# Routing of a mixture-of-experts layer: two-byte lookup tables with the choices innermost, totals taken as one more rank, and the first four gathers issued by the routing block

## The reference

```python
def _L0_ffn_ref(x, W_gate, b_gate, W_e, b_e):
    TOP_K = 2
    logits = x @ W_gate + b_gate
    _, top_idx = jax.lax.top_k(logits, TOP_K)
    y_all = jax.nn.relu(jnp.einsum('bsd,edh->bseh', x, W_e) + b_e)
    y = jnp.take_along_axis(y_all, top_idx[..., None], axis=2)
    return y.mean(axis=2)
...
x = x + 0.5 * _L0_ffn_ref(_layernorm(x, axis=-1), ...)
x = x + _L0_attn_ref(_layernorm(x, axis=-1), ...)
x = x + 0.5 * _L0_ffn_ref(_layernorm(x, axis=-1), ...)
```

## Time and profile before

| | |
|---|---|
| median of 3 runs | 1069.3 us (1067.76 to 1070.01) |
| the profiled execution, its time | 1067.34 us |
| the profiled execution, its span in the trace | 1065.6 us |
| first expert layer in the trace: routing, experts | 0 to about 105 us, about 106 to about 240 us |
| second expert layer: routing, experts | about 784 to 912 us, 913 us to the end |
| TensorE busy over the span | 82% |
| granted TensorE clock, mean | 0.918 of full |

### The profile page before, as it was taken

One profiled execution on the slowest core, in us unless ns is written; L12 is line 12 of the kernel. 1 busy time (PEld: TensorE's weight loads), 2 busy tenths in 40 slices (PEclk: granted clock), 3 DMA queues, 4 the chain that ended last, 5 costly groups with the idle time before them and its releaser, 6 DMA issues. The chain is left out here.

```text
span 1065.6 us, 20204 instructions
## 1 busy us (share of the span) xinstructions
PE 876.0 (82%) x6688; PEld 640.8 (60%) x6689; DVE 670.0 (63%) x1295; ACT 443.9 (42%) x817; POOL 355.4 (33%) x340
## 2 busy tenths in 40 slices
PE   3676799993699987838999999999959984699994
PEld 3564688872477776725555555555437863488873
DVE  7977244431788988837777777777527676344431
ACT  3332233331134433334777777777723430133331
POOL 5540677764012321220000000000014440477764
PEclk9997799997799999977999999999979895699997
DMA  8873578863226488664666666554047882378773
GB/s 262 284 261 119 163 143 150 149 120 62 46 85 188 149 217 203 164 201 119 146 147 136 135 138 138 132 137 119 25 134 245 291 277 99 75 141 158 145 134 49
DMA packets 123099, 162.08 MB, mean 152 GB/s; under 512 B 16864, under 2 KB 74336, under 8 KB 122752
## 3 DMA queue, kind: packets, MB, share of 16 engines
q1 hardware_dynamic: 105168, 123.85, 41.5%
q0 software_dynamic: 17856, 37.25, 18.8%
HBM read 97.44 MB, written 67.37 MB: 155 GB/s over the span
## 5 line engine op out<-in xcount | busy, mean ns | idle before, releaser
L825 DVE TENSOR_REDUCE att_part<-att_s_ps 128x2 f32<-128x1024 f32 (+2 forms) x160 | 195.5, 1225 | 67.4 <-PE att_s_ps L673 67.0
L787 ACT ACTIVATE att_prob<-att_st_ps 128x512 f32<-128x512 f32 x320 | 173.7, 595 | 78.4 <-PE att_st_ps L699 78.0
L143 PE MATMUL exp_z_ps<-ex_w_hi,exp_xT_hi 128*128 x312 | 132.7, 425 | 3.4 <-issue 2.1
L144 PE MATMUL exp_z_ps<-ex_w_lo,exp_xT_hi 128*128 x312 | 126.0, 404 | 0.0
L145 PE MATMUL exp_z_ps<-ex_w_hi,exp_xT_lo 128*128 x312 | 125.7, 403 | 0.0
L1459 DVE TENSOR_TENSOR exp_xT_lo<-exp_t_ps,exp_xT_hi 128x512 fp32r<-128x512 f32 x78 | 54.0, 692 | 109.3 <-ACT exp_xT_hi L1445 109.3
L1452 ACT ACTIVATE exp_y<-exp_y 128x512 f32<-128x512 f32 x72 | 45.5, 632 | 170.5 <-DVE exp_y L1471 170.5
L1387 POOL DMA_INDIRECT exp_xg<-xn,ex_token_of x78 | 77.9, 999 | 89.5 <-SPq L1359 61.4
L1094 POOL TENSOR_TENSOR ex_w_lo<-ex_bias,ex_w_hi 128x1024 fp32r<-128x1024 f32 x32 | 75.8, 2368 | 90.0 <-ACT ex_w_hi L1198 89.9
L712 PE MATMUL att_pv_ps<-att_prob,att_v_sb 128*32 128x256 f32 (+2 forms) x1280 | 101.4, 391 | 1.8 <-ACT att_oT L792 1.8
L637 POOL CAST att_m_parts<-att_part 128x28 fp32r<-128x28 f32 x32 | 6.6, 206 | 271.5 <-DVE att_part L829 271.5
(11 more groups left out here) (198 smaller groups left out, 1725.1 us busy)
## 6 DMA issues: line engine op xcount, KB each, us to landing
ex_bias<-in_L_ffn_W_e SPq DMA_DIRECT2D x32, 512.0 KB, 6.5
v_vals<-qkv_vals SPq DMA_DIRECT2D x16, 512.0 KB, 2.8
q_parts<-qkv_partq SPq DMA_DIRECT2D x32, 256.0 KB, 3.3
k_parts<-qkv_partk SPq DMA_DIRECT2D x32, 256.0 KB, 3.7
att_v_sb<-v_vals SPq DMA_DIRECT2D x32, 256.0 KB, 3.5
ex_bias<-in_L_attn_hidden_states SPq DMA_DIRECT2D x8, 512.0 KB, 4.1
acc<-ex_bias SPq DMA_DIRECT2D x8, 512.0 KB, 6.5
xn<-route_xn SPq DMA_DIRECT2D x8, 512.0 KB, 4.9
```

The source lines that it names most:

```text
L143: nc.tensor.matmul(out, x_hi[:, s], w_hi(c), start=(c == 0), stop=False)
L144: nc.tensor.matmul(out, x_hi[:, s], w_lo(c), start=False, stop=False)
L787: nc.scalar.activation(prob[n % 2][:, col:col + 512], st_ps[(e + half) % 3][:, :], ACT.Exp).then_inc(exp_done, 1)
L825: nc.vector.tensor_reduce(out, src, X_AXIS, ALU.max, negate=True).then_inc(red_done, 1)
```

## The change

- The two tables have all operands in two-byte elements and the 32 choices as the innermost index. `at_tile` is written by three operations of VectorE on two tensors each; its second part is preset by POOL with the tiles' numbers. `at_col` is written by 4 operations of 1024 elements (8 choices each) in place of 32 of 128. PE's 32 matmuls read every 32nd element of `at_tile` and every 8th of `at_col`, and wait once for 8 of them.
- The totals are no longer 16 matmuls of their own: the rank matmuls run one tile further.
- `token_of` is written right behind the matmuls and ahead of `before_of`. POOL issues gathers 0 to 3 at the end of the routing block, from `ex.gather`; the expert block starts at gather 4.
- The identity is built once, and the six `prime` transfers are issued in the routing block, ahead of the first `w_lo`.
- `xn` of the routing block and the first four gather buffers share the memory `ex.rows`. `at_col` lies in the idle `wo_turned` in the first layer and in `o` and `xT` in the second.

```diff
@@ class Experts
+        self.rows = m.sb("rows", [P, C, D]) if rows is None else rows
+        self.ident = m.sb("ident", [P, P])
+        self.prime = m.sb("prime", [1, ADD_RING * 16])
...
+    def gather(self, nc, xn_dram, s, xg):
+        nc.gpsimd.indirect_dma_start(out=xg, out_offset=None, in_=xn_dram[:, :],
+                                     in_offset=bass.IndirectOffsetOnAxis(ap=self.token_of[:, s:s + 1], axis=0)
+                                     ).then_inc(self.gathered[s % ADD_RING], 16)
@@ route_block, gpsimd
-            nc.gpsimd.iota(n_col[:, :], [[1, P]], channel_multiplier=0, **small).then_inc(const_done, 1)
+            nc.gpsimd.iota(n_col[:, :, :], [[1, P], [0, COLS]], channel_multiplier=0, **small).then_inc(const_done, 1)
+            nc.gpsimd.iota(at_tile[:, 1, :, :], [[1, TAB], [0, 2 * TILES]], channel_multiplier=0, **small).then_inc(const_done, 1)
...
+            for r in range(ADD_RING):
+                nc.gpsimd.dma_start(ex.prime[0:1, r * 16:(r + 1) * 16], ident[0:1, 0:16]).then_inc(ex.added[r], 16)
+            for r in range(ADD_RING):
+                pool.wait_ge(ex.added[r], 16)
             for n in range(TILES):
                 pool.wait_ge(w_hi_done, n + 1)
...
+            pool.wait_ge(tr_done, TILES)
+            for par in range(2):
+                pool.wait_ge(xn_stored[par], 16 * (PAIRS // 2))
+            pool.wait_ge(token_done, 1)
+            for s in range(C):
+                ex.gather(nc, xn_dram, s, ex.rows[:, s, :])
@@ route_block, tensor
+            nc.tensor.matmul(total_ps, ones_bf[:, :], both[:, 0:2 * E], start=False, stop=False, skip_group_check=True)
             for s in range(1, TILES):
-                last = nc.tensor.matmul(rank_ps[:, s * 2 * E:TE2], ones_bf[:, :], both[:, 0:TE2 - s * 2 * E], start=False,
-                                        stop=(s == TILES - 1), skip_group_check=True)
-            for s in range(TILES):
-                last = nc.tensor.matmul(total_ps, ones_bf[:, :], both[:, s * 2 * E:(s + 1) * 2 * E],
-                                        start=(s == 0), stop=(s == TILES - 1))
+                last = nc.tensor.matmul(route_ps[:, s * 2 * E:TE2 + 2 * E], ones_bf[:, :], both[:, 0:TE2 - (s - 1) * 2 * E],
+                                        start=False, stop=(s == TILES - 1), skip_group_check=True)
...
             for n in range(2 * TILES):
-                pe.wait_ge(onehot_done, n + 1)
-                nc.tensor.matmul(id_ps, at_col[:, n % COL_RING, :], at_tile[:, n, :, :].rearrange("p a s -> p (a s)"),
-                                 start=(n == 0), stop=(n == 2 * TILES - 1)).then_inc(ids_done, 1)
+                if n % COLS == 0:
+                    pe.wait_ge(onehot_done, n // COLS + 1)
+                last = nc.tensor.matmul(id_ps, at_col[n // COLS][:, :, n % COLS],
+                                        at_tile[:, :, :, n].rearrange("p a s -> p (a s)"), start=(n == 0), stop=(n == 2 * TILES - 1))
+            last.then_inc(ids_done, 1)
@@ route_block, vector
-            chain(nc.vector.tensor_tensor(at_tile[:, :, 0, :], slot_hi[:, :, :].to_broadcast(every),
...
-            for n in range(2 * TILES):
-                if n >= COL_RING:
-                    dve.wait_ge(ids_done, n - COL_RING + 1)
-                nc.vector.tensor_scalar(at_col[:, n % COL_RING, :], n_col[:, :], slot_lo[:, n:n + 1], None,
-                                        ALU.is_equal).then_inc(onehot_done, 1)
+            chain(nc.vector.tensor_tensor(at_tile[:, 0, :, :], at_tile[:, 1, :, :], by_choice(slot_hi[:, :], TAB), ALU.is_equal))
+            chain(nc.vector.tensor_tensor(at_tile[:, 1, :, :], at_tile[:, 0, :, :], by_choice(n_token_row[:, :], TAB), ALU.mult))
+            chain(nc.vector.tensor_tensor(at_tile[:, 2, :, :], at_tile[:, 0, :, :], by_choice(n_token_tile[:, :], TAB), ALU.mult))
+            for j in range(2 * TILES // COLS):
+                nc.vector.tensor_tensor(at_col[j], n_col[:, :, :],
+                                        by_choice(slot_lo[:, j * COLS:(j + 1) * COLS], P), ALU.is_equal).then_inc(onehot_done, 1)
...
+            dve.wait_ge(ids_done, 1)
+            chain(nc.vector.tensor_copy(found[:, :, :], ids))
+            nc.vector.scalar_tensor_tensor(ex.token_of[:, :], found[:, 2, :], float(P), found[:, 1, :],
+                                           ALU.mult, ALU.add).then_inc(token_done, 1)
@@ expert_block, gpsimd
-            gather(0)
-            make_identity(nc, pool, ident, zeroed, ident_done)
-            for s in range(1, AHEAD):
+            for s in range(C, AHEAD):
                 gather(s)
```

82 lines of the change are left out of this document (36 added, 46 removed).

## The result

The changed kernel takes 1078.15 us (median of 4 runs, 1076.38 to 1079.51); the kernel before took 1069.19 in the same session. The ratio is 1.0096, with a 95% interval of 1.0070 to 1.0121: slower, where I had forecast 1063.8 and a gain. The profiled execution has a span of 1076.1 us against 1065.6, so 10.5 us are to be explained.

A forecast was written before the change was run, and what follows sets the result against it. Bound: routing's serial VectorE-TensorE-VectorE chain, then TensorE in the expert block. Layer one -3.2 - 1.95 + 2.2 = -2.95, layer two -3.2 + 0.6 = -2.6, together -5.5: profiled 1067.3 to 1061.8, median 2.0 above, 1063.8; range 1058.5 to 1069.

The forecast's parts named there:

- Only then does POOL reach the barrier ... With the old 1.29 TensorE enters at 6.5.: Routing's end: fourth gather issued 5.2 us after `token_of`, barrier 1.29 later; first expert product z at 9.1, both layers.
- used to share the queues with the 2 MB of biases: Layer one, `token_of` to first expert product z: gathers formerly shared queues with biases; 9.1 against 11.05 us gains 1.95.
- Half of it gives 12.5 for the first `w_lo` ... So 2.8 - 0.57 = 2.2 reach the gate.: Layer one start: half the 2.6 us queue congestion delays priming; fourth weight load 2.8 late, 2.2 us lost.
- ScalarE's slack: Layer one start: ScalarE's copy of the last tile but one started 0.57 us after rounding, subtracted from the 2.8 delay.
- Neither row is near, so I take the middle, 0.165.: TensorE's 32 table matmuls with strided operands: 0.165 us each, between 0.103 packed and 0.228 for four-byte transposes.
- the upper row: Upper price for the 32 matmuls: transposes of 128 four-byte columns at the same 0.50 clock, 0.228 us each.
- T to `token_of`: Start of the tables (T) to `token_of` written: 9.45 us in place of 12.43, in each layer.
- strided reads cost as four-byte ones: Rival on the 32 matmuls: 0.228 us each, 2.0 more per layer, 1067.8 in all; chance 0.10.
- hide behind POOL's gathers: Behind `token_of`, VectorE's `before_of` operations and `row_of` take about 3 us, covered while POOL issues gathers.
- VectorE's terms: Tables on VectorE: three `at_tile` operations at 0.82 us each, 2.6 in all; four `at_col` at 0.72 with gap.
- T+3.3: Tables: the first of four `at_col` operations is done 3.3 us after their start, and the 32 matmuls begin.
- the totals, -0.2: Logits to tables, each layer: 256 columns added to the rank matmuls and 16 matmuls gone, 0.2 us less.

The follow-up runs named there:

- one gather: Changed kernel with only gather 0 in the routing block, gathers 1 to 3 at the start of the expert block; 1069.61 us in a single run.
- `iota`s: Changed kernel with four 128 x 480 number writes by GpSimd where the four gathers were issued, all first gathers in the expert block; 1078.57 us, one run.
- no bias load: Changed kernel with layer one's 2 MB bias load issued by SyncE at the start of the expert block, behind the barrier; 1071.65 us, one run.
- the gathers put back: Changed kernel with gathers 0 to 3 issued at the start of the expert block again; 1074.01 us, ratio 1.0062 to the kernel before.
- both loads put back: Changed kernel with the six priming transfers behind the `w_lo` operations and all first gathers in the expert block; 1068.97 us, ratio 1.0026 to the kernel before.
- both loads put back and `before_of` moved: Kernel with both loads put back, and the five `before_of` operations ahead of VectorE's wait for the 32 matmuls; 1067.76 us, ratio 1.0018 to the kernel before.

## Why the prediction was wrong

The span came out 16.0 us above the forecast (+10.5 against -5.5). Three steps failed. They make 16.7 us in these two traces, and the rest of the table takes 0.7 back.

**"Only then does POOL reach the barrier ... With the old 1.29 TensorE enters at 6.5."** This is the largest, 7.3 + 2.7 = 10.0 us over the two layers. I took the issue of the last gather for the end of GpSimd's block. The block ended only when its transfers had landed: 4.05 us after the end of the last issue, not 1.29. That is 2.7 per layer, which is what layer two missed by (11.78 against 9.1) and layer one too once the bias load is away (11.83). In layer one I had argued that the gathers would gain because they "used to share the queues with the 2 MB of biases". They still did: the load waits for the last 16 transposes, ended at 110.04, and was issued at 110.08, while gather 1 was. Another 4.6. That the barrier waits for the landings of GpSimd's own transfers is shown by three runs (one gather: 3.67; `iota`s: 2.09 and 1.75; no bias load: 4.10 and 4.10) and by the packets: in six kernels with gathers in front of the barrier it opened 1.55 to 1.76 us behind their last packet, in both layers of each. A transfer of SyncE's queue did not hold it: before, the bias load was issued at 104.38 and its packets ran until 111.40, over the barrier at 106.30, and so it was with the gathers put back. Which wait in the block's end does it, the profile does not show.

**"Half of it gives 12.5 for the first `w_lo` ... So 2.8 - 0.57 = 2.2 reach the gate."** Mechanism right, size wrong: 6.1, 3.9 more, in this trace. Over the six kernels with this start it is 2.6 to 6.1 against the one trace of before, 4.3 in the mean, so about 2 of the 3.9 repeat and the rest may be luck. The first `w_lo` began at 13.65, 1.15 later than I said: GpSimd was free at 6.69 and not 6.0, six issues took 3.2 and not 3.0, and the last landing 3.76 more and not 3.5. The fourth weight load came at 18.31 against 14.52, so 3.8 late and not 2.8. That is 1.0 of the 3.9; the other 2.9 is what followed. The delay did not travel unchanged to the last load, as I had it, but grew on the way, to 5.1 at the fifth (23.62 against 18.52) and 6.4 at the last (75.42 against 69.06); the logits were 6.1 late, so ScalarE's slack took 0.3 off it and not 0.57. SyncE's queue stood behind its wait, the transfer engines were idle for 4 us, and VectorE waited 20.1 us for inputs where it had waited 4.3. That the idle transfer engines are why the delay grew fits these rows, but no run isolates it. The `iota`s, on which 2.4 us of my delay rested, cost nothing where the priming doesn't stand behind them, although `n_col` took 1.92 and not 1.0: GpSimd then waits 1.92 us for the weights.

**"Neither row is near, so I take the middle, 0.165."** The matmuls cost 0.208, between my price and the upper row (0.228). That is 1.4 us per layer, and it explains all of the miss in T to `token_of` (10.86 against 9.45; VectorE's part agreed). My rival "strided reads cost as four-byte ones" (0.228) was the nearest. I had also treated both operands alike; only the moving one counts for the pace. The Trainium skill (Advanced Engine Details and Errata, Memory Cachelines) pointed the right way with its lines of 16 bytes and the two hits that full speed needs: a column every 64 bytes has one hit in a line, one every 4 bytes has four, and the trace agrees with it, 0.205 against 0.099 us. For the weights the trace shows no such penalty on the pace: their step of 16 bytes is a new line each time too, and the matmul takes 0.098 us.

What was said of `before_of` and `row_of`, that they "hide behind POOL's gathers", held only because those gathers held the barrier longer. Once the gathers are gone VectorE's chain ends the block in layer two and costs 1.6; in layer one the 16 transposes end it. I had not asked what stands behind the 32 matmuls on TensorE's own queue.

Right were VectorE's terms: 0.82 and 0.83 for `at_tile` (forecast 0.82), 0.61 from start to start for `at_col` (forecast 0.72, so a little better), the start of the matmuls at T+3.3, and the totals, -0.2 in layer two. The Trainium skill (VectorE: DVE Perf Modes, the perf-mode tier table) gives two elements a cycle for `tensor_tensor` on two-byte data; the trace agrees: 1280 elements in 0.82 us, against 1.49 before with a broadcast innermost. In layer one logits to T came out 1.2 shorter; the 15 rank matmuls with the totals took 1.10 us there. So they did with both loads put back (stretch 11.22) and with the `iota`s for gathers (11.23); in the kernel with only the priming moved, where the stretch is 12.19, they took 1.96; the granted clock reads 1.00 around them in both. Why, I have not settled, but kernels with the same code there show either, so it takes no change of the code.

Open: in the trace with both loads put back and `before_of` moved, what the change touches adds up to less than before: z of layer one at 114.55 against 115.09, and in layer two 12.18 + 10.80 + 7.96 = 30.9 from logits to z against 33.3. Yet its ratio is 1.0018, with an interval down to 0.9996. In that trace z to end took 150.67 instead of 146.26; in the changed kernel and the other variants it took 146.7 to 148.5, in every one more than before. Whether that is chance or comes from the expert block's changed buffers I have not tried.

## What to carry to other kernels

In this kernel a block's end waits for the landing of the transfers that GpSimd issued in it: an early transfer in front of such a barrier pays only if it lands before the slowest engine arrives, and a large transfer beside it can put the landing off, here by 4.6 us. A layout that makes one engine's innermost dimension contiguous can break the other's: look for one that serves both, as pairs of two-byte elements do, and measure the stride that no row shows with eight matmuls before pricing it. Before adding a wait at a start-up, ask which queue stands behind it and whether the transfer engines go idle: here 4 idle us came with a loss of 2.6 to 6.1. And look at a stretch in more than one trace before calling its difference the change's.

## What the runs showed of the hardware

- A matmul of 128x120 two-byte columns at a granted clock of 0.50 takes 0.096 us packed, 0.099 with a column every 4 bytes, and 0.205 with one every 64 bytes; weights read with a step of 16 bytes do not change the pace (0.098).
- GpSimd passed the barrier 3.96 to 4.10 us after the issue of the last of its four gathers, 3.58 to 3.67 after a single one, and 7.06 to 9.07 with a 2 MB load beside four; each time 1.55 to 1.76 us after the gathers' last packet. With none of its transfers in flight it was 1.25 to 1.66 us after the last engine's last instruction, with a 2 MB load of SyncE's queue in flight or not.
- VectorE's `tensor_tensor` on two-byte data keeps 0.82 us for 1280 elements when only two elements are contiguous and one operand is broadcast above them.
- Behind 32 matmuls at a granted clock of 0.50 the 16 transposes ran at 0.99 and took 1.94 us in one trace, at 0.65 and 2.92 in another with the same 32 matmuls of 0.10 us, and at 0.50 to 0.62 and 3.04 to 3.59 behind 32 of 0.21 us. The shorter chain alone does not settle the clock.
